# Latent attention with the keys on partitions, one group of 32 rows per head, and denominators from a ones column

## What is computed

```python
c_q = x @ W_DQ                                   # 64 latent channels
Qc, Qr = c_q @ W_UQ, rope(c_q @ W_QR)            # 16 heads of 16 and of 8
c_kv = x @ W_DKV                                 # 64 latent channels
Kc, V = c_kv @ W_UK, c_kv @ W_UV                 # 16 heads of 16
Kr = rope(x @ W_KR)                              # 8 channels, the same for all heads
scores = clip([Qc, Qr] @ [Kc, Kr].T, -80, 80)    # 24 channels a head, causal
weights = softmax(scores / sqrt(24))
x = x + (weights @ V) @ W_O                      # x inside is layernorm(x)
```

## Time and profile before

| what | value |
|---|---|
| time, median of 3 runs | 897.19 us (897.19 to 898.05) |
| the profiled execution | 897.43 us |
| its span in the trace | 895.6 us |
| PE busy, weight loads busy | 763.5 us, 510.2 us |
| DVE, ACT, POOL busy | 570.1 us, 429.0 us, 316.5 us |
| mean granted clock of TensorE | 0.92 |
| stage p9 ends, a3 starts on PE | 782.99 us |
| a3 ends (last add: 824.46 + 0.69) | 825.15 us |

### The profile page before, as it was taken

One profiled execution on the slowest core, in us unless ns is written; L12 is line 12 of the kernel. 1 busy time (PEld: TensorE's weight loads), 2 busy tenths in 40 slices (PEclk: granted clock), 3 DMA queues, 4 the chain that ended last, 5 costly groups with the idle time before them and its releaser, 6 DMA issues. The chain is left out here.

```text
span 895.6 us, 19146 instructions
## 1 busy us (share of the span) xinstructions
PE 763.5 (85%) x7000; PEld 510.2 (57%) x7000; DVE 570.1 (64%) x1295; ACT 429.0 (48%) x1281; POOL 316.5 (35%) x380
## 2 busy tenths in 40 slices
PE   6999999697999999967777299999388896777996
PEld 5788887444433333345456288888267773365334
DVE  3565556539699999976795533232697775465484
ACT  3756666462574665235365100000368882755572
POOL 2211121027477887731351350100564431233002
PEclk9999999798699999989898599999689997979899
DMA  8111700000020000000001036552465310000001
GB/s 260 38 41 53 271 14 1 2 1 1 23 72 0 1 1 1 0 1 0 2 2 48 25 129 179 182 156 72 145 200 195 100 37 1 1 3 3 0 1 49
DMA packets 44893, 51.79 MB, mean 58 GB/s; under 512 B 7072, under 2 KB 40832, under 8 KB 44544
## 3 DMA queue, kind: packets, MB, share of 16 engines
q1 hardware_dynamic: 40256, 43.48, 15.4%
q0 software_dynamic: 1536, 4.20, 1.6%
q10 hardware_dynamic: 3008, 2.88, 0.9%
HBM read 45.31 MB, written 5.24 MB: 56 GB/s over the span
## 5 line engine op out<-in xcount | busy, mean ns | idle before, releaser
L968 PE MATMUL r_u_ps<-r_t_in,l_same_head 128*128 128x512 f32 x124 | 69.4, 641 | 1.0
L936 POOL TENSOR_TENSOR r_q_in<-r_state,rec_q 128x512 f32<-128x512 f32 x62 | 68.1, 1098 | 0.0
L1374 ACT ACTIVATE a_prob<-a_s_ps,a_negmax 128x256 f32<-128x256 f32 x128 | 59.2, 488 | 17.7 <-DVE a_negmax L1436 17.7
L1755 ACT ACTIVATE a_prob<-a_s_ps,a_negmax 128x256 f32<-128x256 f32 x128 | 58.7, 485 | 18.3 <-DVE a_negmax L1791 18.3
L2352 PE MATMUL m_h_ps<-m_rowsT,l_w 128*128 128x256 f32 x256 | 58.7, 390 | 0.0
L1442 DVE COPY a_probT<-a_w_ps 128x512 f32<-128x512 f32 x48 | 31.4, 687 | 39.0 <-PE a_w_ps L1290 39.0
L2352 PEld LDWEIGHTS m_h_ps<-m_rowsT,l_w 128*128 128x128 f32 x256 | 50.2, 197 | 7.3
L2363 PE MATMUL m_y_ps<-l_w,m_hidden 128*128 128x256 f32 x240 | 53.9, 379 | 0.0
L2398 ACT ACTIVATE m_rowsT<-m_xt_ps,l_B_s,l_B_g 128x256 f32<-128x256 f32 x16 | 8.2, 561 | 93.1 <-PE m_xt_ps L2340 93.1
L2266 DVE TENSOR_SCALAR m_hidden<-m_h_ps,l_b 128x256 f32<-128x256 f32 x64 | 28.0, 479 | 37.8 <-PE m_h_ps L2352 37.8
L1791 DVE TENSOR_REDUCE a_negmax<-a_s_ps 128x2 f32<-128x512 f32 x64 | 40.9, 681 | 17.1 <-PE a_s_ps L1671 17.1
(11 more groups left out here) (388 smaller groups left out, 1899.9 us busy)
## 6 DMA issues: line engine op xcount, KB each, us to landing
l_w<-in_B_w SPq DMA_DIRECT2D x16, 1024.0 KB, 5.9
a_ctxT<-in_ctxT SPq DMA_DIRECT2D x31, 256.0 KB, 2.9
a_ctx<-in_ctx SPq DMA_DIRECT2D x16, 256.0 KB, 2.7
expert_out<-m_y ACTq DMA_DIRECT2D x7, 256.0 KB, 5.8
all_X<-in_x SPq DMA_DIRECT2D x4, 256.0 KB, 5.4
l_b<-in_B_b SPq DMA_DIRECT2D x1, 1024.0 KB, 6.6
all_xnT<-own_rows SPq DMA_DIRECT2D x1, 1024.0 KB, 5.5
routed_rows<-ffn_xn SPq DMA_DIRECT2D x8, 128.0 KB, 1.8
```

What stands on the lines that cost most here:

```text
L936: ins = nc.gpsimd.tensor_tensor(q_in[i % 2][m][:, :, :, :], twice(state[i % 2][m]), steps("q", 2 * i - 1, 2, m), ALU.mult)
L968: nc.tensor.matmul(u_ps[m][:, :, :, :], same_head[:, :], t_in[m][:, :, :, :], start=False, stop=True).then_inc(u_mm[m], 1)
L1374: ins = nc.scalar.activation(prob[n % 2][:, r, m, :], s_ps[r][:, m, :], ACT.Exp, bias=negmax[n % 2][:, r, m:m + 1], accum_out=den[n % 2][: ...
L1755: ins = nc.scalar.activation(prob[n % 2][:, r, m, :], s_ps[r][:, m, :], ACT.Exp, bias=negmax[n % 2][:, r, m:m + 1], accum_out=den[n % 2][: ...
```

## The change

In p9, D_up gets 768 columns in place of 512: the heads' channels of queries and keys are laid out so that each head has 32 columns, of which 16 hold its channels and 16 are zero. `channels(c, g)` now runs for 4 groups g of 4 heads and both chunks, 8 times, at the end of PE's queue: a query matmul (L2481) and a key matmul (L2482) as before, and a third one (L2485) that adds the rotary query to rows 16 to 23 of each head's 32, with a 0/1 matrix `pick` of 128 x 512. ACT copies each query bank (8 in place of 4). DVE takes each key bank with one add of the rotary key (L2554, 8 in place of 8 multiplications). `place_keys` is gone, `take_values` is one copy in place of four, with a ones column beside each head's 16 values, which POOL sets (L2581) in place of the large memset.

In a3, `latent_attention_stage` replaces the shared stage. The keys are the stationary operand, so that scores come out with 64 keys on partitions by 64 queries (L2631), one matmul a head. The exponentials go as they are, as stationary operand, into the values' matmul with 17 moving columns (L2644), whose 17th result is the denominator. DVE takes reciprocals (L2718) and divides the rows (L2720), PE turns the rows (L2652, 2 transposes a tile in place of 8), ACT copies them (L2689), PE applies W_O (L2660), DVE adds (L2724). The last unit's second tile is turned and multiplied in banks of the scores. POOL has nothing left to do there. On SP, one load of 256 KB (D_pick) takes the place of two of 1 and 2 KB, and D_up's load grows from 256 to 384 KB.

The diff, cut to its core:

```diff
-            for m in range(KD):
-                uses += [(("q", c, m), (q_ready, ONE + KD * c + m + 1)), (("k", c, m), (k_ready, ONE + KD * c + m + 1))]
             for i in range(2):
                 uses += [(("qr", c, i), (qr_taken, ONE + 2 * c + i + 1)), (("v", c, i), (v_ready, ONE + 2 * c + i + 1))]
+        for c in range(2):
+            for g in range(4):
+                uses += [(("q", c, g), (q_ready, ONE + 4 * c + g + 1)), (("k", c, g), (k_ready, ONE + 4 * c + g + 1))]
...
-                def channels(c, m):
-                    cols = slice(c * N, (c + 1) * N)
-                    q_acc, k_acc = free_bank("q", c, m), free_bank("k", c, m)
-                    nc.tensor.matmul(q_acc[:, :], up_w[upper, m * P:(m + 1) * P], lowT[upper, cols], start=True, stop=True).then_inc(q_mm, 1)
-                    nc.tensor.matmul(k_acc[:, :], up_w[lower, m * P:(m + 1) * P], lowT[lower, cols], start=True, stop=True).then_inc(k_mm, 1)
+                def channels(c, g):
+                    cols, out = slice(c * N, (c + 1) * N), slice(g * P, (g + 1) * P)
+                    q_acc, k_acc = free_bank("q", c, g), free_bank("k", c, g)
+                    nc.tensor.matmul(q_acc[:, :], up_w[upper, out], lowT[upper, cols], start=True, stop=False)
+                    nc.tensor.matmul(k_acc[:, :], up_w[lower, out], lowT[lower, cols], start=True, stop=True).then_inc(k_mm, 1)
+                    if g == 0:
+                        pe.wait_ge(qr_ready, ONE + c + 1)
+                    nc.tensor.matmul(q_acc[:, :], pick[:, out], q_rope[:, cols], start=False, stop=True).then_inc(q_mm, 1)
...
-                    pe.wait_ge(low_ready, ONE + c + 1)
-                    for m in range(KD):
-                        channels(c, m)
                     if c == 0:
                         normed.turn(pe, 6)
                         normed.turn(pe, 7)
+                    pe.wait_ge(low_ready, ONE + c + 1)
                     for i in range(2):
                         rotary_and_values(c, i)
+                for c in range(2):
+                    for g in range(4):
+                        channels(c, g)
...
-                    nc.scalar.activation(QT[:, m, c * N:(c + 1) * N], bank("q", c, m)[:, :], ACT.Copy).then_inc(q_ready, 1)
+                def take_queries(c, g):
+                    act.wait_ge(q_mm, ONE + 4 * c + g + 1)
+                    nc.scalar.activation(queries[:, g, c * N:(c + 1) * N], bank("q", c, g)[:, :], ACT.Copy).then_inc(q_ready, 1)
 
                 def take_values(c, i):
                     act.wait_ge(v_mm, ONE + 2 * c + i + 1)
-                    act.wait_ge(zeroed, ONE + 1)
-                    for e in range(2):
-                        for b in range(2):
-                            first = 8 * c + 4 * i + b
-                            ins = nc.scalar.activation(vblk[e * T:(e + 1) * T, first:first + 3:2, :, e * HD:(e + 1) * HD],
-                                                       bank("v", c, i)[b * T:(b + 1) * T, :].rearrange("p (t h e d) -> p t h e d", t=2, h=HH, e=2)[:, :, :, e, :], ACT.Copy)
-                    ins.then_inc(v_ready, 1)
-
-                def place_keys(c, e):
-                    act.wait_ge(kr_sum, ONE + c + 1)
-                    nc.scalar.activation(k_rope[:, c * HB:(c + 1) * HB, e, :], plain_k[c][:, :, :], ACT.Copy, scale=quad[:, e:e + 1]).then_inc(kr_ready, 1)
+                    nc.scalar.activation(vals[:, 4 * c + 2 * i:4 * c + 2 * i + 2, :, 0:HD], bank("v", c, i)[:, :].rearrange("p (t h d) -> p t h d", t=2, d=HD), ACT.Copy).then_inc(v_ready, 1)
...
-                def take_keys(c, m):
-                    dve.wait_ge(k_mm, ONE + KD * c + m + 1)
-                    for e in range(2):
-                        ins = nc.vector.tensor_scalar(keys[:, m, c * HB:(c + 1) * HB, e, :], bank("k", c, m)[:, :].rearrange("p (b s) -> p b s", s=T), par[:, e:e + 1], None, ALU.mult)
-                    ins.then_inc(k_ready, 1)
+                def take_keys(c, g):
+                    dve.wait_ge(k_mm, ONE + 4 * c + g + 1)
+                    if g == 0:
+                        dve.wait_ge(kr_sum, ONE + c + 1)
+                    nc.vector.tensor_tensor(keys[:, g, c * N:(c + 1) * N], bank("k", c, g)[:, :], plain_k[c][:, :], ALU.add).then_inc(k_ready, 1)
...
-                nc.gpsimd.memset(vblk[:, :, :, :], 0.0).then_inc(zeroed, 1)
+                nc.gpsimd.memset(vals[:, :, :, HD:HD + 1], 1.0).then_inc(ones_set, 1)
...
+def latent_attention_stage(nc, stage, X, queries, keys, vals, ident, WoT, limit, scale):
+    NU = NT // 2
+    with Scope(nc, stage) as sc:
+        shifted = [sc.sb(f"shifted{r}", [P, 8, T]) for r in range(4)]
+        prob = [[sc.sb(f"prob{j}{r}", [P, 8, T]) for r in range(4)] for j in range(2)]
+        rden = sc.sb("rden", [P, 2, H])
+        rows = [sc.sb(f"rows{i}", [P, H, HD]) for i in range(2)]
+        headsT = sc.sb("headsT", [P, 2, KD, P])
+        s_ps = [sc.ps(f"s_ps{r}", [P, 8, T]) for r in range(4)]
+        o_ps = [sc.ps(f"o_ps{i}", [P, H, 32]) for i in range(2)]
+        turned_ps = sc.ps("turned_ps", [P, 2, KD, P])
+        out_ps = sc.ps("out_ps", [P, 2, D])
...
+        def turned_at(u, i):
+            return s_ps[0][:, 0:2 * KD, :].rearrange("p (k a) t -> p k (a t)", k=KD) if u == NU - 1 and i == 1 else turned_ps[:, i, :, :]
+        def out_at(u, i):
+            return s_ps[1][:, 0:4, :].rearrange("p g t -> p (g t)") if u == NU - 1 and i == 1 else out_ps[:, i, :]
+        with sc.block() as block:
+            @block.tensor
+            def _(pe):
+                def scores(u):
+                    if u >= 1:
+                        pe.wait_ge(shifted_ready, ONE + 4 * u)
+                    for i in range(2):
+                        for g in range(4):
+                            for j in range(2):
+                                b = 4 * u + 2 * i + j
+                                for r in range(4):
+                                    group = slice(32 * r, 32 * r + 32)
+                                    mm = nc.tensor.matmul(s_ps[r][64 * j:64 * j + 64, 4 * i + g, :], keys[group, g, b * T:(b + 1) * T], queries[group, g, b * T:(b + 1) * T], start=True, stop=True)
+                                    if i == 1 and g == 3 and j == 1:
+                                        mm.then_inc(s_mm, 1)
+                def values(u, i):
+                    if u >= 1:
+                        pe.wait_ge(rows_ready, ONE + 2 * (u - 1) + i + 1)
+                    for r in range(4):
+                        pe.wait_ge(exp_done, ONE + 4 * u + r + 1)
+                        for g in range(4):
+                            for j in range(2):
+                                half = slice(64 * j, 64 * j + 64)
+                                mm = nc.tensor.matmul(o_ps[i][half, 4 * g + r, 0:HD + 1], prob[u % 2][r][half, 4 * i + g, :], vals[half, 2 * u + i, 4 * g + r, :], start=True, stop=True)
+                    mm.then_inc(pv_mm, 1)
+                def turn(u, i):
+                    pe.wait_ge(rows_ready, ONE + 2 * u + i + 1)
+                    if u >= 1 and i == 0:
+                        pe.wait_ge(heads_ready, ONE + 2 * u)
+                    for k in range(KD):
+                        mm = nc.tensor.transpose(turned_at(u, i)[:, k, :], rows[i][:, 8 * k:8 * k + 8, :].rearrange("p h d -> p (h d)"), ident[:, :])
+                    mm.then_inc(turned, 1)
+                def output(u, i):
+                    pe.wait_ge(heads_ready, ONE + 2 * u + i + 1)
+                    if u >= 1 and i == 0:
+                        pe.wait_ge(x_added, ONE + 2 * u)
+                    for k in range(KD):
+                        mm = nc.tensor.matmul(out_at(u, i), headsT[:, i, k, :], WoT[:, k, :], start=(k == 0), stop=(k == KD - 1))
+                    mm.then_inc(out_mm, 1)
+                scores(0)
+                for u in range(NU):
+                    if u + 1 < NU:
+                        scores(u + 1)
+                    values(u, 0)
+                    values(u, 1)
+                    for i in range(2):
+                        if u >= 1:
+                            output(u - 1, i)
+                    for i in range(2):
+                        turn(u, i)
+                for i in range(2):
+                    output(NU - 1, i)
+            @block.scalar
+            def _(act):
+                def exps(u, r):
+                    act.wait_ge(shifted_ready, ONE + 4 * u + r + 1)
+                    if u >= 2:
+                        act.wait_ge(pv_mm, ONE + 2 * (u - 1))
+                    nc.scalar.activation(prob[u % 2][r][:, :, :], shifted[r][:, :, :], ACT.Exp, scale=scale).then_inc(exp_done, 1)
+                def take_heads(u):
+                    act.wait_ge(turned, ONE + 2 * u + 2)
+                    if u >= 1:
+                        act.wait_ge(out_mm, ONE + 2 * u)
+                    nc.scalar.activation(headsT[:, :, :, :], turned_ps[:, :, :, :], ACT.Copy).then_inc(heads_ready, 2)
...
+            @block.vector
```

(28 more changed lines are left out.)

121 lines of the change are left out of this document (64 added, 57 removed).

## The result

The changed kernel takes 911.64 us (median of 4 runs, 908.71 to 912.95) against 897.6 us (4 runs, 897.19 to 898.05): a ratio of 1.0152, 95% interval 1.0125 to 1.0179. It is 14 us slower. In a later series the same kernel gave 915.26 us (6 runs, 908.53 to 917.83) beside 897.71 us, 1.0195 (1.0168 to 1.0222). Its ten runs spread over 9 us, where those of the kernel before (23 in that series) spread over 6; what lies behind that is seen in the clock.

The account below looks back on a forecast made before the run. PE was taken to set the time in latent inputs and the new attention. 897.43 + 7.5 (latent inputs) - 3.6 (attention) + 4.5 (low clock) = 905.8 profiled, 905.5 median; own range 901 to 910, with rivals 894 to 917.

Parts of the forecast that it names:

- half a stretch: Low end of the 901 to 910 range: half of one 11.5 us low-clock stretch in the attention; two at the top.
- Latent inputs: Stage before the attention: eight triples of 1.92 us make the attention start at 790.5, +7.5 us.
- 0.1 for changing between half and whole array: Latent inputs: estimated 0.1 us for array-shape changes within each triple of 1.92 us.
- The idle tail: Before the attention: values and rotary keys move beside the triples, so 5 us of idle PE fall to about 1.
- Attention at the full clock: Attention stage, PE setting the time: a sum of 38.55 us against 42.16, -3.6 us.
- The values: Attention: 128 records a unit at 29.5 ns, 3.78 us a unit, 15.1 us in all.
- the 0.8 us for changes of array shape: Attention: an estimated 0.8 us over the whole stage, part of its 38.55 us.
- The clock: Attention: the clock falls once for an 11.5 us stretch, from loads with little streaming behind them; +4.5 us.
- A: Rival: the clock stays up in the attention, 901.1 us; chance 0.14.
- B: Rival: values' records cost 17 ns, 894.7 us with the clock up, 899 if it falls; chance 0.24.
- C: Rival: the values' two quarters take turns, 59 ns a record, +15.1, 916 us with the clock up; chance 0.07.
- D: Rival: a floor of 25 ns a record under the short score matmuls, +4.8, 910 us; chance 0.03.

Follow-up runs that it names:

- the filled head: Three unread 128x512 matmuls added to the changed kernel while PE waits for the first clamps of the attention; median 911.24 us.
- the small pick: Changed kernel with the rotary-query matmul using only its group's 32 non-zero rows, two side by side; 907.64 us, 1.0119 to the kernel before.
- the filled idle time: Kernel before with five unread 128x512 matmuls in PE's 5 us of idle time ahead of the attention; 896.37 us, ratio 0.9988.
- four do: Changed kernel with sequences reordered so the values' matmuls go round all four 64x64 quarters of the array; 897.55 us, 1.0004 to the kernel before.
- the two improvements: Changed kernel with both the rotary-query matmuls on 32 rows, side by side, and the values on four array quarters; 897.08 us, 0.9991 to the kernel before.

## Why the prediction was right, and where it was off

The sign, and with 911.64 us the stated range, held; the forecast's own range of 901 to 910 did not, and 905.5 is 6 us short. (Its lower end of 901 is the sum with no low clock at all, not with "half a stretch".) Two errors of opposite sign stand in the sum, and that they partly cancel is luck: the attention at the full clock was costed about 2.9 us too high, and the clock 6 to 11 us too low.

**Latent inputs: right.** +7.5 was forecast, +8.2 measured. "0.1 for changing between half and whole array" was too little: the triples are 2.11 us apart instead of 1.92, 1.5 us over eight, since the two changes cost 0.39 together. The idle tail went as said, 0.94 us of idle PE ahead of the first scores, and the rest of the stage came out 0.9 us shorter than summed.

**Attention at the full clock: a little better than the sum.** The values were costed at 29.5 ns a record; 30.5 was measured over a whole unit, 29.2 from start to start. That the price came out so well was in part a guess: it was taken from loads onto two column halves of the whole array. The scores went faster than the 2.0 us a unit, 1.58, so the halved columns did count. No run shows the 0.8 us for changes of array shape by itself. Between the two profiles of the changed kernel 13.6 us of low clock made 5.8 us of time; taken back to none from the second, 46.0 - 24 x 0.43 = 35.7 us (an estimate), against the 38.55 of the sum and the 42.16 of before.

**The clock: this step failed, in its size, and its mechanism held in part.** "I expect the clock to fall once in the attention for a stretch like the old one" gave +4.5. It fell once for 24 us in one profile and three times for 37 in the other, 10 and 16 us by the estimate above. The mechanism, loads with little streaming behind them, fits the later falls, at 820.7 and 830.9, which lie in the values, and the filled head, where the clock fell 2.5 us into them. It does not fit the first fall elsewhere: in every other profile of the new design that comes ahead of the first values, by 0.6 and 1.2 us in the two of the changed kernel and by 3.6 with the small pick, where PE has only the short scores and waits of about 1 and 2.5 us. The prediction had put the idle time aside as a cause. The filled head shows that the wait isn't needed for a fall, not that it has no part in it; and 32 columns in place of 17 left the stretch at 24 us. The size was taken from a stretch of the old kernel, where other work followed after 11.5 us. Here slow work of the same kind goes on, and PE, which is busy 23.5 of the 23.7 us of the first stretch, passes nearly all of it on: 0.43 us for each us of low clock. In the old kernel it doesn't: half of PE's 8.92 busy us was my price, and with 4.7 us less of low clock behind the filled idle time the attention was 1.1 us shorter, 0.23 for each us (an estimate from one profile each).

With the terms as they turned out, 897.6 + 8.2 - 6.5 (35.7 - 42.16) and 10 to 16 us for the clock give 909.6 to 915.3 us, which is where the medians of the two series lie.

**The rivals.** A (clock up) didn't come. B asked for 17 ns a record; two quarters don't reach it, four do (16 ns), and then the kernel is where the old one was, near the 899 that B gave for a clock that falls as well. C (quarters take turns, 59 ns) is refuted by 30.5 ns, and by the records of the two quarters, which start 7 ns apart. By the Trainium skill's rule on row tiles and one bank ("TensorEngine Tiling (Array Packing)", section "Restrictions and Gotchas") the two would have to take turns; two row tiles that write different partitions of one bank did not, and sharing it cost nothing: a quarter takes a record every 58 ns with it and without it. D is refuted: 128 records of 64 columns in 1.58 us are 12.3 ns each, half of the floor of about 25 ns for 1 to 64 columns that the Trainium skill names ("TensorE: Matmul & The Clock Gate", "Back-to-back issue gap"). Here the matmuls run side by side on eight tiles of the array.

**Open:** why the two improvements don't add, beyond one profile's clock; how the waits and the values share in bringing the clock down; and whether the load or a fixed price of a matmul makes the 58 ns.

## What to carry to other kernels

A record of a matmul with a handful of moving columns held its quarter of the array for 58 ns, whether 17 or 32 columns moved. So count how many quarters the loop goes round: two gave 30 ns a record, four 16, at the cost of an order of sequences and of 0.8 us in the first unit (0.2 before), in which PE waits for DVE's divisions. Padding from 17 to 32 columns was free, and the kernel was 4 to 6 us faster with it in two series; the clock is the likely reason and not a shown one. And ask of a new schedule not only what it costs at the full clock, but who hides a low one: where PE waited for others, a us of low clock cost 0.23 us, and where it never waited 0.43.

## What was not expected of the hardware

- The clock's low stretches are not the program's alone: two executions of the same kernel had 24 and 37 us of them in the attention, and its runs spread from 908.5 to 917.8 us.
- PE stops for 0.3 to 1.5 us inside a series of short matmuls, with nothing to wait for that the profile's rows show ("issue"). The place goes by the count of PE's instructions: nine profiles of the changed design have it 27 records into the third unit's values; without the eight picks (16 records fewer) it is at 43, and with three more matmuls (6 records) in the head at 21. What PE waits for is very likely its own instructions. The trace has a queue that moves instructions, in packets of 16 KB:

```profile
q8 instruction: 58, 0.95, 0.4%
```

All 18 such stops in the fourteen profiles, the kernels before and with 32 columns among them, end 1.2 to 1.5 us after a packet of this queue has landed, and most packets are followed by no stop. With two quarters the stop in the third unit is 0.45 to 0.9 us, with four 0.99, 1.30 and 1.53, in the order in which the packet ahead of it took 0.96, 1.01 and 1.28 us. So short matmuls that run side by side can outrun the loading of their own code; no experiment tried it. The longest one:

```profile
815.70 1.70 PE L2650 MATMUL a_o_ps<-mla_vals,a_prob 64*64 64x17 f32 x101 [1.53 <-issue]
```

- Two matmuls of 512 columns on two groups of 32 rows, into two banks, took the time of one (1.13 us for four records).
